# Node units from both ends, scatters gated on a count of written units, 18 ticks after the last stage

## The reference, cut to what matters

```python
x = x + relu(attention aggregation of h[src], h[dst], edge features into dst)   # L0
x = x + (fc(h) * out_deg^-0.5)[src] summed into dst, * in_deg^-0.5, + h         # L1
x = x + two graph convolutions with self loops, + h                             # L2
x = x + relu(two graph convolutions with self loops + h)                        # L3
```

## Time and profile before

| | |
|---|---|
| median of 3 runs | 2444.54 us (2444.05 to 2446.86) |
| span of the profiled execution | 2443.7 us (no other time of it is given) |
| PE busy | 1785.7 us, 73% |
| DVE busy | 1845.2 us, 76% |
| ACT busy | 1377.4 us, 56% |
| POOL busy | 1781.6 us, 73% |
| mean granted TensorE clock | 0.877 of full speed |

### The profile page before, as it was taken

One profiled execution on the slowest core, in us unless ns is written; L12 is line 12 of the kernel. 1 busy time (PEld: TensorE's weight loads), 2 busy tenths in 40 slices (PEclk: granted clock), 3 DMA queues, 4 the chain that ended last, 5 costly groups with the idle time before them and its releaser, 6 DMA issues.

```text
span 2443.7 us, 26381 instructions
## 1 busy us (share of the span) xinstructions
PE 1785.7 (73%) x6414; PEld 872.1 (36%) x6414; DVE 1845.2 (76%) x3016; ACT 1377.4 (56%) x3086; POOL 1781.6 (73%) x1776
## 2 busy tenths in 40 slices
PE   3888888874998588878999878868999788860000
PEld 1333333322444244334444334434444344430000
DVE  6999998746888488986999688886999799960000
ACT  2766676632887365546888655546888666620000
POOL 6777777776777777736777577756777577777776
PEclk9999999986999799978999888988999899975555
DMA  3344443224776354434444356654444455440000
GB/s 71 90 124 129 127 123 97 71 75 132 233 240 216 115 182 128 133 115 107 129 131 130 102 167 188 184 170 115 128 130 129 112 139 136 129 133 22 23 21 20
DMA packets 223229, 302.24 MB, mean 124 GB/s; under 512 B 78896, under 2 KB 85165, under 8 KB 222952
## 3 DMA queue, kind: packets, MB, share of 16 engines
q1 hardware_dynamic: 166632, 249.64, 31.3%
q0 software_dynamic: 56448, 50.92, 11.6%
HBM read 156.13 MB, written 144.91 MB: 123 GB/s over the span
## 4 chain that ended last, share of the span: by engine, by line
DVE 23%; POOL 21%; issue 14%; PE 10%; ACT 6%; DMA 1%; DVEq 0%; POOLq 0%; SPq 0%; ACTq 0%
POOL mn_ring L529 13%; POOL out_dram L1889 8%; DVE node_h L1407 5%; PE bank L1197 5%; DVE mn_total L1581 4%; DVE node_x L1431 2%; DVE node_h L1452 1%; DVE mn_ring L1566 1%; ACT node_square L1326 1%; DVE node_mean L1414 1%; DVE mn_scaled L1597 1%; ACT node_std L1310 1%; PE bank L1206 1%; PE bank L1201 1%; PE bank L1191 1%
## 5 line engine op out<-in xcount | busy, mean ns | idle before, releaser
L529 POOL DMA_INDIRECT mn_ring<-slot_rows,addr_i x980 | 976.8, 997 | 390.4 <-issue 295.5
L1197 PE MATMUL bank<-node_x,center 128*128 128x512 f32 x492 | 250.8, 624 | 97.0 <-DVE node_h L1407 92.7
L1326 ACT ACTIVATE node_square<-bank 128x512 f32<-128x512 f32 x246 | 145.9, 593 | 222.6 <-PE bank L1197 222.6
L1201 PE MATMUL bank<-node_square,mean 128*128 128x512 f32 x492 | 265.5, 622 | 3.4 <-ACT node_std L1305 2.7
L1206 PE MATMUL bank<-node_h,wconv 128*128 128x512 f32 x492 | 266.1, 624 | 0.3 <-DVE mn_sums L1719 0.3
L529 POOL DMA_INDIRECT found<-node_table,look_i x196 | 209.7, 1070 | 74.9 <-issue 62.8
L529 POOL DMA_INDIRECT xin<-in_x_dram,src_i x192 | 195.2, 1017 | 64.3 <-issue 57.6
L529 POOL DMA_INDIRECT xin<-in_x_dram,dst_i x192 | 196.5, 1023 | 58.5 <-issue 58.5
L1889 POOL DMA_INDIRECT out_dram<-keep,scat_i x196 | 193.1, 985 | 62.5 <-issue 62.5
L1211 PE MATMUL bank<-node_act,wconv 128*128 128x512 f32 x442 | 230.9, 605 | 1.9 <-ACT node_act L1320 1.9
L1320 ACT ACTIVATE node_act<-bank,bias 128x512 f32<-128x512 f32 x246 | 170.5, 693 | 86.0 <-PE bank L1206 86.0
(11 more groups left out here) (337 smaller groups left out, 3807.0 us busy)
## 6 DMA issues: line engine op xcount, KB each, us to landing
out_dram<-node_rows SPq DMA_DIRECT2D x98, 256.0 KB, 3.4
mn_rin<-res SPq DMA_DIRECT2D x96, 256.0 KB, 3.6
slot_rows<-node_rows SPq DMA_DIRECT2D x96, 256.0 KB, 2.1
slot_rows<-keep SPq DMA_DIRECT2D x96, 256.0 KB, 2.3
mn_fcol<-f_rows SPq DMA_DIRECT2D x192, 128.0 KB
res<-mn_x SPq DMA_DIRECT2D x72, 256.0 KB, 3.0
node_x_in<-in_x_dram SPq DMA_DIRECT2D x64, 256.0 KB, 3.0
mn_ring<-slot_rows,addr_i POOLq DMA_INDIRECT x980
```

The source lines that it names most:

```text
L529: return eng.indirect_dma_start(out=dest, out_offset=None, in_=table, in_offset=bass.IndirectOffsetOnAxis(ap=index, axis=0))
L1197: pe.matmul(bank[i][:, :], C["center"][:, :], src, start=True, stop=True).then_inc(s["centered"][i], 1)
L1201: pe.matmul(bank[4][:, :], C["mean"][:, :], nd.square[:, i - 1, :], start=True, stop=True) \
L1326: act.activation(nd.square[:, i - 1, :], bank[i][:, :], ACT.Square).then_inc(s["squared"][i], 1)
```

## The change

Four things are changed.

1. The tick table: `SHARE` and `GAP` are smaller and the last tick is moved from group 20 of F to behind group 24 of F. The stages A to F now have 22, 13, 24, 13, 24 and 34 ticks, of which the last 18 (ticks 112 to 129) stand behind the last group of F. `AHEAD` falls from 34 to 22 units, so 76 units have their norm in their own tick instead of 64.
2. Node units are taken from both ends of the nodes in turn (`node_first`), as the edge tiles are.
3. POOL no longer waits for all units ahead of the scatters. DVE works out for each pair of tiles how many units must have been written (`covers`, seven small instructions in the look-up chain at the end of A, from the last row of the destinations, which SP copies into `reach` in the front phase). POOL loads that number at five places of the scatters (groups 0, 17, 20, 22 and 24, each for all groups up to the next place) and waits until the count of units copied for output has reached it. ACT adds four to the count when the last writes have landed.
4. The wait of the last unit's write for the one before it becomes a wait of the fourth unit's write for the second one's, since those two now overlap.

```diff
-SHARE = dict(A=1.0, B=0.72, C=1.0, D=0.72, E=1.0, F=1.05)
-GAP = dict(A=2, B=2, C=2, D=2, E=2, F=0)
+SHARE = dict(A=1.0, B=0.5, C=1.0, D=0.5, E=1.0, F=0.8)
+GAP = dict(A=0, B=2, C=2, D=2, E=2, F=0)
+CLEAR = (16, 19, 21, 23, GROUPS - 1)
...
-        upto = TICKS if (st, g) == ("F", GROUPS - 5) else min(int(due), TICKS)
+        upto = TICKS if (st, g) == ("F", GROUPS - 1) else min(int(due), TICKS)
...
+def node_first(u):
+    i = u - LOCALS
+    unit = i // 2 if i % 2 == 0 else NODE_UNITS - 1 - i // 2
+    return min(unit * UR, N - UR)
...
+                sp.dma_start(C["reach"][:, :], C["dst"][P - 1:P, :]).then_inc(s["reach"], 16)
...
-        if u == n - 1:
-            sp.wait_ge(s["stored"][(i - 1) % 4], 16 * (LOCALS + (i - 1) // 4 + 1))
+        if i == 3:
+            sp.wait_ge(s["stored"][1], 16 * (LOCALS + 1))
...
+                def covers():
+                    pairs = far[0:1, :].rearrange("o (q h) -> o q h", h=2)
+                    link(v.tensor_scalar(far_i[0:1, :], C["reach"][:, :], 10, None, ALU.logical_shift_right))
+                    link(v.tensor_copy(far[0:1, :], far_i[0:1, :]))
+                    link(v.tensor_scalar(low[0:1, :], pairs[:, :, 0], 2.0, 1.0, ALU.mult, ALU.add))
+                    link(v.tensor_scalar(high[0:1, :], pairs[:, :, 1], -2.0, 2.0 * NODE_UNITS, ALU.mult, ALU.add))
+                    link(v.tensor_tensor(low[0:1, :], low[0:1, :], high[0:1, :], ALU.max))
+                    link(v.tensor_scalar(low[0:1, :], low[0:1, :], float(NODE_UNITS), 4.0, ALU.min, ALU.add))
+                    link(v.tensor_copy(C["cover"][:, :], low[0:1, :]))
+                    mark["cover"] = done[0]
...
                         mark[name] = done[0]
+                        if lo == 0:
+                            covers()
...
-                for k in range(4):
-                    gp.wait_ge(nd.s["stored"][k], 16 * (LOCALS + (NODE_UNITS - k + 3) // 4))
+                gp.wait_ge(s["late"], mark["cover"])
+                clear = iter(CLEAR)
+                upto = -1
                 for g in range(n):
+                    if g > upto:
+                        upto = next(clear)
+                        q = upto * GP + pairs_of(upto) - 1
+                        units = gp.value_load(C["cover"][0:1, q:q + 1], min_val=5, max_val=NODE_UNITS + 4)
+                        gp.wait_ge(nd.s["out_rows"], units)
+                        gp.sem_inc(s["open"], 1)
+                        gp.wait_ge(s["open"], CLEAR.index(upto) + 1)
                     send(g)
...
+                for i in range(NODE_UNITS, NODE_UNITS + 4):
+                    act.wait_ge(nd.s["stored"][i % 4], 16 * (LOCALS + i // 4))
+                    act.activation(ended[0:1, i - NODE_UNITS:i - NODE_UNITS + 1], C["eps"][0:1, 0:1], ACT.Copy).then_inc(nd.s["out_rows"], 1)
```

More of the change, by code:

```diff
@@ L168, in build @@
             r_open=sb("r_open", [1, KP]), r_nopen=sb("r_nopen", [1, KP]),
+            reach=sb("reach", [1, TILES], I32), cover=sb("cover", [1, HQ], I32),
             same=sb("same", [P, HE], U8), keep=sb("keep", [P, COLS]))
@@ L571, in front_phase @@
                  "mean cent squared var lnv rstd factor hh h1_t hd_t e_t h1T hdT e0T e1T msg logits msg_out logit_out klog:2 "
-                 "u_in:3 u_kept:3 umean ucent usq uvar ulnv urstd ufactor uh u_x2")
+                 "u_in:3 u_kept:3 umean ucent usq uvar ulnv urstd ufactor uh u_x2 reach")
         s.update(H["landed"])
@@ L635, in load_units @@
                     for j in range(2):
-                        first = min((AHEAD[2 * g + j] - LOCALS) * UR, N - UR)
+                        first = node_first(AHEAD[2 * g + j])
                         sp.dma_start(unit_rows(xu[:, g % 3, j * W:j * W + W]),
@@ L696, in _ @@
                 sp.wait_ge(s["looked"], 16 * LOOK_FRONT)
+                sp.wait_ge(s["reach"], 16)
             @block.gpsimd
@@ L1127, in rows_of @@
     def rows_of(self, a, u):
-        first = min((u - LOCALS) * UR, N - UR)
+        first = node_first(u)
         return a[first:first + UR, :].rearrange("(p r) f -> p r f", r=UR // P)
@@ L1482, in main_phase @@
         unit = ctx.enter_context(nc.sbuf_tensor("mn_unit", [1, 1], F32))
+        far_i = ctx.enter_context(nc.sbuf_tensor("mn_far_i", [1, TILES], I32))
+        far = ctx.enter_context(nc.sbuf_tensor("mn_far", [1, TILES], F32))
+        low = ctx.enter_context(nc.sbuf_tensor("mn_low", [1, HQ], F32))
+        high = ctx.enter_context(nc.sbuf_tensor("mn_high", [1, HQ], F32))
+        ended = ctx.enter_context(nc.sbuf_tensor("mn_ended", [1, 4], F32))
         keep = C["keep"]
         s = sems(nc, ctx, "mn", "kv_in:2 aux_in:2 res_in:3 x_kept:3 fetched:4 gs turned total joined fcol_in:2 scaled product "
-                 "mixed back part x mean cent squared var lnv rstd h row res stored h_kept:2 sent looked looked_last late late_pe so_kept")
+                 "mixed back part x mean cent squared var lnv rstd h row res stored h_kept:2 sent looked looked_last late late_pe so_kept open")
         def w_of(g):
```

## The result

The changed kernel takes 2429.01 us (median of 4 runs, 2426.42 to 2430.6) against 2445.7 us of the kernel before beside it (2444.05 to 2446.97): a ratio of 0.9928, 95% interval 0.9916 to 0.994. The forecast was 2429, a change of -15 us; measured are -16.7. In the profiled execution the span fell from 2443.7 to 2427.1 us.

A forecast was written before the change was run, and what follows sets the result against it. POOL's queue plus four stage-border waits was taken to bound the kernel. Terms -6 (front), -11 (B's border), -1 (B, D), -4 (F's ring), +5 (loads), +2 (stretch) sum to -15 us: 2429, forecast 2418 to 2439, whole range 2408 to 2447.

The forecast's parts named there:

- POOL's queue bounds the time: From front phase to end, time is POOL's queue plus four stage-border waits, 90.0 us together; ticks matter only where they delay POOL.
- R1: Rival: the 18 ticks moved behind F were on the path, so all 152 us come off, 2292 us; 3%.
- Front phase, -6 us: Front phase: six groups lose their unit pair, 1.05 us of POOL's gathers each, 6 us less; bounds 4 and 8.
- Border behind B, -11 us: Wait of C's first gather: scan 24's lag falls from 22 to 11 us, the wait from 36.3 to 25; bounds 7 and 14.
- B and D, -1: Gathers of stages B and D: fewer ticks mean slightly fewer stretched gathers, 1 us less for both together.
- D's border, C and E, nothing: Behind D scan 24's lag is 9.8 us already; C and E keep 24 ticks and their pace: no change.
- F's ring, -4: Stage F: the ring ran dry four times, 4.0 us; with 16 ticks it doesn't, 4 us less.
- Loads, +5: Scatters: POOL's five register loads of the unit count cost 1 us each, 5 us more; bounds 1.5 to 20.
- The five gaps of 1 to 2 us: Sign among the scatters: they stay about 1.3 us apart, with five gaps of 1 to 2 us.
- Stretch, +2: Scatters beside the 18 ticks behind F are slowed by DVE work: 2 us more, 4 if all 0.24 a tick counts.
- R4: Rival, scatters: four two-SBUF-input vector instructions a tick delay a scatter 0.37 us each, 27 us instead of 2, 2454; 7%.
- R5: Rival, stages B and D: PE idles more and its clock falls to half, up to +96 us, 2525; slower at 5%.

## Why the prediction came out right, point by point

*POOL's queue bounds the time.* Right, and shown from both sides: 132 us of work beside the scatters went with a gain of 16.7 us, five more ticks moved gave none, and the same 18 ticks cost 132 us as soon as POOL had to wait for them. R1, ticks on the path, is out.

*Front phase, -6 us.* The mechanism was right, the size was not: -2.5 in the profile. Over all profiles, B's first gather comes at 812.2 to 813.2 us with 17 pairs and at 807.1 to 810.7 with 11, on average 3.7 apart, and the gathers of the front phase alone take 4.3 less. That is 0.6 to 0.7 us a pair, the lower bound of the forecast (0.70, the overlap of L938 alone). The trace shows this bound itself: each of the 17 pairs of the kernel before, and each of the 11 of the changed one, stretches one gather, by 0.69 to 0.72 us (12.0 and 7.9 us in all), and no second gather is delayed by the reduction behind the addition. The error was the value chosen between the bounds: two long windows were compared, and the whole difference of 1.05 us a group was put down to the pairs.

*Border behind B, -11 us.* -12.6. Scan 24 now lags 9.7 us behind the gathers (forecast 10.6, before 22). The side remark that the two ticks behind A are part of the late end is not borne out: put back beside the smaller share, they change nothing.

*B and D, -1; D's border, C and E, nothing.* -2.2 for the gathers of B and D, -1.3 for the other borders, each of the size by which repeats differ.

*F's ring, -4.* -4.3, of which 3.1 are waits: the gathers of F still wait for PE three times, 0.9 us in all, where none was forecast. The run with B's share alone shows it from the other side: F with a full tick in each of 21 groups waits 12.8 us.

*Loads, +5.* Nothing, even for 25. The issue gap of 0.30 us stays between the scatters; the lower bound, 0.3 a load, was still too much. The price was taken as if POOL did one thing after the other. That it loads and waits during the scatter ahead would explain the nothing, but the trace has no row for a load, so this is argued. The five gaps of 1 to 2 us that were named as a sign are not there.

*Stretch, +2.* +6.5. The forecast averaged over stage E, where a tick and its groups run at another beat. That left out that the two queues can fall into step. R4 had four instructions a tick at 0.37 us each; it is one at 0.51 and one at 0.18, for nine ticks of 18. The Trainium skill ("SBUF — State Buffer", in "SBUF: two separate sides") calls the port pair that VectorE and GpSimd share an exclusive lock: a VectorE instruction with two SBUF inputs or a GpSimd one that reads SBUF, whichever starts first, has it for the whole instruction, and the other fully blocks. The traces agree for a VectorE instruction that is first: 1.49 us when the addition is ahead by 0.06 us. They don't for a scatter that is first: the additions that start 0.1 us into one take their usual 0.69 us, and only those 0.03 us ahead of one take longer themselves, 0.75.

*R5, the clock.* Right to weigh low. Over the gathers of each stage the granted clock fell in B from 0.94 to 0.88 and in D from 0.91 to 0.85, and the pairs of groups still fitted under POOL's 21 us. (PE's last instruction ends 140 us after the last gather, not 170, for the ticks behind F are shorter than charged; nothing waits for them.)

The two wrong terms of the scatters cancel (+5 and +2 for 0 and +6.5), and the front's 3.5 us too many are made good by small gains elsewhere. So the total is nearer than its parts deserve.

What stays open: why a repeat of the same kernel differs by up to 7 us in its span (2427.1 and 2420.3 for the changed kernel). In the account the difference is spread over all stages, 2.0 us at most in any part, with none that stands out.

## What to carry to other kernels

When one queue is full from start to end, work taken out of its shadow gains only what it had cost that queue: here a late last group at a stage's border, a ring run dry, and vector instructions that hold up address generation. Count along that queue, not the work that is moved. And when two periodic queues run side by side, look for the one instruction that holds up the other queue in each period: reading one operand from another memory took 5.7 us off the scatters, a third of what the whole change gave.

## What the runs showed of the hardware that was not expected

- A GpSimd scatter (0.98 us free) takes 1.49 us if a VectorE addition of two 128x512 f32 SBUF tensors (0.69 us) starts 0.06 us ahead of it, and 0.98 us if the same addition starts 0.1 or 0.77 us behind its start; the addition then keeps its 0.69 us. What is left of the VectorE instruction when the scatter starts, less 0.12 us, is what the scatter loses; only an addition 0.03 us ahead cost it nothing and took 0.75 us itself. With one input read from PSUM no scatter lost more than 0.02.
- The same holds of gathers: 0.83 us left of an addition of two 128x1024 tensors (1.22 us) made 1.65 us of 0.95, 17 times out of 17; single-input reductions of the same size (L900), with 1.0 to 1.2 us left, left gathers at 0.95.
- Two such queues lock in step: ticks of 8.45 us and six scatters of 1.287 us (7.72 us) stayed together over nine ticks, and over fourteen where more ticks followed, by 0.73 us of stretch a tick. With ticks of 8.39 us, that have one such addition less, or with the residual addition reading PSUM, thirteen scatters went with two ticks, at 0.05 and 0.16 us of stretch for the two.
- Register loads from SBUF and waits on their value between indirect transfers on GpSimd: 25 of them left the 62.4 us of gaps between 196 scatters as they were.
